# x - mean instead of the normalized x through both FFNs of a macaron block, and POOL's and TensorE's orders around it

## The reference

```python
x = x + 0.5 * ffn(layernorm(x))     # x: 4 x 256 tokens, 512 wide
x = x + attention(layernorm(x))     # 32 query heads, 8 key heads of 128, window of 128, rope
x = x + 0.5 * ffn(layernorm(x))     # the same weights again

layernorm(x) = (x - mean) / sqrt(var + 1e-5)
# ffn(xf), xf: 1024 x 512
probs = softmax(xf @ W_router.T)                 # 8 experts
w     = the two largest probs, divided by their sum, 0 elsewhere
h     = einsum("td,erd->ter", xf, lora_A)        # rank 16
lora  = einsum("ter,eor,te->to", h, lora_B, w) * 2.0
ffn   = xf @ W_base.T + b_base + lora
```

## Time and profile before

| | us |
|---|---|
| median of 3 runs | 746.47 (746.28 to 747.5) |
| the profiled execution | 746.33 |
| its span | 744.6 |
| TensorE busy in it | 717.2 (96%) |
| VectorE busy | 601.0 (81%) |
| ScalarE busy | 413.3 (56%) |
| POOL busy | 396.5 (53%) |
| mean granted TensorE clock | 0.998 of full |

### The profile page before, as it was taken

How to read it: one execution, slowest core, us unless ns; L and a number is a source line. 1 busy time by engine, 2 the same in 40 slices (tenths; PEclk the granted TensorE clock), 3 DMA queues, 4 the chain that set the end, 5 groups by cost and what they waited for, 6 DMA issues and landing times.

```text
span 744.6 us, 13949 instructions
## 1 busy us (share of the span) xinstructions
PE 717.2 (96%) x3692; PEld 603.1 (81%) x3692; DVE 601.0 (81%) x2060; ACT 413.3 (56%) x1122; POOL 396.5 (53%) x466
## 2 busy tenths in 40 slices
PE   8899789999999999999999999999999999998998
PEld 5787667888888888888888888888888888887786
DVE  6898778877887888878887888788878887788795
ACT  3324475657655676556655766576656665754320
POOL 0674268634864477438653765367535863462420
PEclk9999999999999999999999999999999999999999
DMA  8240003100220022002200120013000310030002
GB/s 266 73 158 16 0 3 98 43 1 2 73 70 1 0 70 70 0 0 70 56 14 0 56 70 14 0 32 94 15 0 0 99 28 1 1 114 1 0 31 85
DMA packets 25843, 32.13 MB, mean 43 GB/s; under 512 B 5833, under 2 KB 14281, under 8 KB 25298
## 3 DMA queue, kind: packets, MB, share of 16 engines
q1 hardware_dynamic: 25232, 30.69, 13.1%
q10 hardware_dynamic: 578, 1.05, 0.4%
HBM read 27.54 MB, written 4.19 MB: 43 GB/s over the span
## 4 chain that ended last, share of the span: by engine, by line
PE 70%; DVE 20%; issue 5%; ACT 3%; DMA 1%; POOL 1%; DVEq 0%; SPq 0%; ACTq 0%
PE bank L1102 26%; PE bank L1160 19%; PE bank L1145 6%; PE bank L1124 5%; PE bank L1068 5%; PE bank L1132 3%; DVE prob L822 2%; DVE rot L787 2%; DVE oT_lo L834 2%; DVE prob L814 1%; DVE sm L807 1%; PE bank L1121 1%; DVE rot L778 1%; ACT prob L550 1%; DVE pT_hi_lo L828 1%
## 5 line engine op out<-in xcount | busy, mean ns | idle before, releaser
L368 POOL TENSOR_TENSOR swap<-swap,rope 128x512 f32<-128x512 f32 x80 | 110.1, 1377 | 129.8 <-ACT swap L523 129.8
L550 ACT ACTIVATE prob<-sm,nmax 128x128 f32<-128x128 f32 x128 | 51.5, 403 | 151.4 <-DVE prob L814 150.4
L375 POOL TENSOR_SCALAR_AFFINE_SELECT pT_hi_lo<-pT_hi_lo 128x256 fp32r<-128x256 f32 x128 | 52.3, 409 | 140.3 <-DVE pT_hi_lo L828 139.8
L523 ACT ACTIVATE swap<-bank 64x512 f32<-64x512 f32 x160 | 94.9, 593 | 10.6 <-PE bank L1102 6.7
L558 ACT ACTIVATE pT_hi_lo<-bank 128x256 fp32r<-128x256 f32 x128 | 48.9, 382 | 71.5 <-PE bank L1132 50.6
L822 DVE TENSOR_SCALAR prob<-prob,rinv 128x128 f32<-128x128 f32 x256 | 83.3, 367 | 4.5
L385 POOL TENSOR_TENSOR q_lo<-rot,q_hi 128x512 fp32r<-128x512 f32 x64 | 82.6, 1291 | 6.9 <-ACT q_hi L531 6.9
L1160 PE MATMUL bank<-wo_hi,oT_hi 128*128 128x512 f32 x256 | 74.6, 413 | 5.0 <-DVE x L841 5.0
L828 DVE TENSOR_TENSOR pT_hi_lo<-bank,pT_hi_lo 128x256 fp32r<-128x256 f32 x128 | 53.6, 418 | 29.4 <-ACT pT_hi_lo L558 29.2
L1102 PE MATMUL bank<-xnT_hi,wq_hi 128*128 128x512 f32 x256 | 71.4, 391 | 2.2 <-DVE v_lo L798 1.4
L1102 PE MATMUL bank<-xnT_lo,wq_hi 128*128 128x512 f32 x256 | 73.4, 389 | 0.0
(11 more groups left out here) (150 smaller groups left out, 1768.9 us busy)
## 6 DMA issues: line engine op xcount, KB each, us to landing
raw<-in_L_attn_wq SPq DMA_DIRECT2D x32, 256.0 KB, 3.0
raw<-in_L_attn_wo SPq DMA_DIRECT2D x32, 256.0 KB, 2.6
x<-in_L_attn_x SPq DMA_DIRECT2D x4, 512.0 KB, 7.3
raw<-in_L_attn_wk SPq DMA_DIRECT2D x8, 256.0 KB, 2.7
raw<-in_L_attn_wv SPq DMA_DIRECT2D x8, 256.0 KB, 2.6
out<-x SPq DMA_DIRECT2D x8, 256.0 KB, 2.0
raw<-in_L_ffn_W_base ACTq DMA_DIRECT2D x4, 256.0 KB, 5.1
wb_keep_hi<-q_hi SPq DMA_DIRECT2D x1, 1024.0 KB, 4.9
```

The lines of the kernel that those rows point to most:

```text
L368: nc.gpsimd.tensor_tensor(w, w, tab, ALU.mult).then_inc(t2_done, 1)
L523: last = nc.scalar.activation(swap[a:a + half, m % 2, :], A[m % 2][b:b + half, :], ACT.Copy)
L550: last = nc.scalar.activation(prob[:, s % 2, lo:hi], src, ACT.Exp, bias=nmax[:, s % 2, i:i + 1], scale=-1.0, accum_out=rsum[:, s % 2, i:i ...
```

## The change

In both FFNs `xn` only subtracts the mean. The inverse deviation, positive for each token, comes back in two places: as the scale of the router's exponential, exp(rstd * (logit - top)), which becomes one activation per tile and waits for POOL's `rstd_done` (`RSTD_AT`), and as the scale of the last operation `ffn_out`. The half that stood there goes into W_base (`scale=0.5` in its copy, and in the low half), and the factor 2 of the LoRA part, halved too, is gone from h. The attention norm is as it was.

With it the orders change. POOL now makes the deviations of tiles 0 and 1 and of 2 and 3 as well, and that of tiles 4 to 7 ahead of the biases of tiles 0 to 3; in the last FFN it makes that of tiles 4 to 7, between the biases of tiles 3 and 4, in VectorE's place. TensorE transposes tiles 0 and 1 of x ahead of W_base, takes dense of pair 0 pass by pass for both tiles (`dense_by_pass`, the two passes with the high half of W_base first), and transposes tiles 2 and 3 ahead of h. VectorE does the statistics of tiles 2 and 3 behind the low half of W_base, and their subtraction ahead of the first router. ScalarE copies W_base in one go behind the x copies.

```diff
@@ -232,6 +232,8 @@
         def wo_lo(g, i):
             return 10 * g + 7 + i
 
+        RSTD_AT = ((1, 2, 3, 3), (6, 7, 8, 8))
+
         def rstd_steps(engine, then, t0, t1):
 
             vr, y, a, b = var[:, t0:t1], rstd[:, t0:t1], nt1[:, t0:t1], nt2[:, t0:t1]
@@ -410,9 +412,11 @@
                             rope_lo(2 * g + hf + 1, split, 1 - hf)
                         weights(g, hf, s, last)
 
+            norm_rstd(0, 0, 2)
+            norm_rstd(0, 2, 4)
+            norm_rstd(0, 4, NT)
             for t in range(NT // 2):
                 bias(0, t)
-            norm_rstd(0, 4, NT)
             split_lo(0, 0, wk_s[0][:, :, :], wk_s[1][:, :, :])
             for i in range(KT):
                 split_lo(1 + i, (1 + i) % RING, wq_s[0][:, i, :], wq_s[1][:, i, :])
@@ -432,6 +436,8 @@
             group(KV - 1, False, True)
             p_part(16 * KV - 1, SLOTS - 1)
             for t in range(NT):
+                if t == NT // 2:
+                    norm_rstd(2, 4, NT)
                 bias(1, t)
 
 
@@ -454,7 +460,7 @@
             def prepare_dense(lo, hi):
                 for d in range(lo, hi):
                     act.wait_ge(prep_tr, 3 + d)
-                    nc.scalar.activation(wb[0][:, d, :], bank[4 + d][:, :], ACT.Copy).then_inc(prep_hi, 1)
+                    nc.scalar.activation(wb[0][:, d, :], bank[4 + d][:, :], ACT.Copy, scale=0.5).then_inc(prep_hi, 1)
 
             def prepare_lora_b():
                 act.wait_ge(prep_tr, 7)
@@ -485,7 +491,11 @@
                 act.wait_ge(esub_done, p + 1)
                 if p == 0:
                     act.wait_ge(preset, 3)
-                nc.scalar.activation(ebuf[:, pr % 2, :, 0:EXPERTS], esub[:, :, :], ACT.Exp).then_inc(e_done, 1)
+                act.wait_ge(rstd_done, RSTD_AT[f][pr])
+                for i in range(2):
+                    t = 2 * pr + i
+                    last = nc.scalar.activation(ebuf[:, pr % 2, i, 0:EXPERTS], esub[:, i, :], ACT.Exp, scale=rstd[:, t:t + 1])
+                last.then_inc(e_done, 1)
 
             def split_hi(n, slot, count, dst):
                 act.wait_ge(raw_landed[slot], 16 * count)
@@ -594,10 +604,9 @@
             act.wait_ge(warm_ready, 1)
             nc.scalar.activation(rsum[:, 0, 0:1], sm[:, 0, 0:1], ACT.Exp)
             prepare_router()
-            prepare_dense(0, KT // 2)
             x_hi(0, 0)
             x_hi(0, 1)
-            prepare_dense(KT // 2, KT)
+            prepare_dense(0, KT)
             for pr in range(NT // 2):
                 if pr == 1:
                     prepare_lora_b()
@@ -679,16 +688,16 @@
                 dve.wait_ge(aggr, NT * ln + t1)
                 rstd_steps(nc.vector, then, t0, t1)
 
-            def norm(ln, t0, t1):
-                for t in range(t0, t1):
-                    norm_stats(ln, t)
-                norm_rstd(ln, t0, t1)
-
             def xn(ln, t):
                 i = NT * ln + t
                 wait(dve, tr_done, i - 1)
-                nc.vector.tensor_scalar(xn_buf(ln, t), x[:, t, :].rearrange("p (a n) -> p a n", a=2), mv[:, t, 0:1], rstd[:, t:t + 1],
-                                        ALU.subtract, ALU.mult).then_inc(xn_done, 1)
+                dve.wait_ge(aggr, i + 1)
+                src = x[:, t, :].rearrange("p (a n) -> p a n", a=2)
+                if ln == 1:
+                    ins = nc.vector.tensor_scalar(xn_buf(ln, t), src, mv[:, t, 0:1], rstd[:, t:t + 1], ALU.subtract, ALU.mult)
+                else:
+                    ins = nc.vector.tensor_scalar(xn_buf(ln, t), src, mv[:, t, 0:1], None, ALU.subtract)
+                ins.then_inc(xn_done, 1)
 
             def x_lo(ln, t):
                 i = NT * ln + t
@@ -731,9 +740,8 @@
                                              einv[:, :].unsqueeze(2).broadcast_to([P, 2, EXPERTS]), ALU.mult))
                 for i in range(2):
                     h = sm[:, i, 0:ER].rearrange("p (e r) -> p e r", e=EXPERTS)
-                    last = nc.vector.scalar_tensor_tensor(
-                        h, h, 2.0,
-                        wgt[:, i, :].unsqueeze(2).broadcast_to([P, EXPERTS, RANK]), ALU.mult, ALU.mult)
+                    last = nc.vector.tensor_tensor(h, h, wgt[:, i, :].unsqueeze(2).broadcast_to([P, EXPERTS, RANK]),
+                                                   ALU.mult)
                 last.then_inc(hw_done, 1)
 
             def ht_lo(f, pr):
@@ -747,7 +755,7 @@
                     t = 2 * pr + i
                     dve.wait_ge(out_done, NT * f + t + 1)
                     dve.wait_ge(biased, NT * f + t + 1)
-                    nc.vector.scalar_tensor_tensor(x[:, t, :], OUTB[f][pr % 2][i][:, :], 0.5, x[:, t, :],
+                    nc.vector.scalar_tensor_tensor(x[:, t, :], OUTB[f][pr % 2][i][:, :], rstd[:, t:t + 1], x[:, t, :],
                                                    ALU.mult, ALU.add).then_inc(x_out, 1)
 
             def prepare_router():
@@ -762,8 +770,8 @@
             def prepare_dense():
                 for d in range(KT):
                     dve.wait_ge(prep_hi, 3 + d)
-                    nc.vector.tensor_tensor(wb[1][:, d, :], bank[4 + d][:, :], wb[0][:, d, :].bitcast(F32),
-                                            ALU.subtract).then_inc(prep_lo, 1)
+                    nc.vector.scalar_tensor_tensor(wb[1][:, d, :], bank[4 + d][:, :], 0.5, wb[0][:, d, :].bitcast(F32),
+                                                   ALU.mult, ALU.subtract).then_inc(prep_lo, 1)
 
             def prepare_lora_b():
                 dve.wait_ge(prep_hi, 7)
@@ -849,7 +857,6 @@
                     dve.wait_ge(sum_done, 5 * 2 * KV)
                     dve.wait_ge(vt_done, 2 * KV)
                 if s in (2, 7):
-                    dve.wait_ge(rstd_done, 5 if s == 7 else 4)
                     xn(2, 2 if s == 7 else 0)
                     xn(2, 3 if s == 7 else 1)
                 if s == 3:
@@ -888,19 +895,19 @@
 
 
             nc.vector.memset(sm[:, 0, :], 0.0).then_inc(warm_ready, 1)
-            norm(0, 0, 2)
+            norm_stats(0, 0)
+            norm_stats(0, 1)
             xn(0, 0)
             xn(0, 1)
             prepare_router()
-            norm_stats(0, 2)
-            norm_stats(0, 3)
             x_lo(0, 0)
             x_lo(0, 1)
             prepare_dense()
-            router(0, 0)
-            norm_rstd(0, 2, 4)
+            norm_stats(0, 2)
+            norm_stats(0, 3)
             xn(0, 2)
             xn(0, 3)
+            router(0, 0)
             prepare_lora_b()
             ht_lo(0, 0)
             x_lo(0, 2)
@@ -913,7 +920,8 @@
                 if pr == 1:
                     router(0, pr)
                 if pr != 2:
-                    dve.wait_ge(rstd_done, 1 + pr // 2)
+                    if ln == 1:
+                        dve.wait_ge(rstd_done, 4)
                     xn(ln, t)
                     xn(ln, t + 1)
                 if pr > 1:
@@ -926,7 +934,7 @@
                     xn(0, 6)
                     xn(0, 7)
                 if ln == 1:
-                    dve.wait_ge(rstd_done, 3)
+                    dve.wait_ge(rstd_done, 5)
                     xn(1, 2)
                     xn(1, 3)
                 if ln == 1:
@@ -948,7 +956,8 @@
             norm_stats(1, NT - 1)
             rope_sum(0, 1)
             rope_cos(0, 2)
-            norm_rstd(1, 4, NT)
+            dve.wait_ge(aggr, 2 * NT)
+            rstd_steps(nc.vector, then, 4, NT)
             xn(1, 4)
             xn(1, 5)
             rope_sum(0, 2)
@@ -982,7 +991,6 @@
             x_add(4 * KV - 1, BATCH - 1, 1)
             norm_stats(2, 6)
             norm_stats(2, 7)
-            norm_rstd(2, 4, NT)
             for pr in range(1, NT // 2):
                 if pr > 1:
                     ht_lo(1, pr - 1)
@@ -1017,6 +1025,8 @@
                     last = tp(bank[3][:, d * EXPERTS:(d + 1) * EXPERTS], rot[0:EXPERTS, 1, d * P:(d + 1) * P],
                               ident[0:EXPERTS, 0:EXPERTS])
                 last.then_inc(prep_tr, 1)
+                x_transpose(0, 0)
+                x_transpose(0, 1)
                 for c in range(OUT // P):
                     pe.wait_ge(w_landed[c], 16)
                     for d in range(KT):
@@ -1067,6 +1077,15 @@
                     a, b = PASSES[n]
                     mm(OUTB[f][pr % 2][i][:, :], xnT[a][:, d, (2 * pr + i) * P:(2 * pr + i + 1) * P], wb[b][:, d, :],
                        start=(n == 0 and d == 0), stop=False)
+
+            def dense_by_pass(f, pr, order):
+
+                for n in order:
+                    a, b = PASSES[n]
+                    for i in range(2):
+                        for d in range(KT):
+                            mm(OUTB[f][pr % 2][i][:, :], xnT[a][:, d, (2 * pr + i) * P:(2 * pr + i + 1) * P], wb[b][:, d, :],
+                               start=(n == 0 and d == 0), stop=False)
 
             def h_transpose(f, pr):
                 p = 4 * f + pr
@@ -1198,19 +1217,17 @@
 
 
             prepare()
```

(8 more changed lines are left out.)

## The result

The changed kernel takes 750.94 us (median of 4 runs, 750.69 to 751.82), the kernel before 746.99 beside it (746.28 to 747.61). The ratio is 1.0050, 95% interval 1.0036 to 1.0065: slower by 0.5%. 747.6 was forecast, with a range that ended at 748.9. The profiled execution took 750.69, span 749.0 against 744.6, so 4.4 us are to be found.

The account below looks back on a forecast made before the run. TensorE was taken to bound the whole run, and POOL's queue to decide the changed front: +1.5 us at the projections and -0.3 at the end gave +1.2, forecast 747.6 us, range 745.0 to 748.9.

Parts of the forecast that it names:

- The step that failed: First FFN: pair 2 to the attention transposes keeps its 11.2 us, so TensorE is through at about 49.7.
- POOL's queue: First FFN: POOL runs without a gap from 27.5 and has the attention norm's first deviation at 52.5 instead of 49.39.
- the subtractions of tiles 6 and 7: First FFN, from 34.4 on: beside POOL's work the two tiles take 2.88 us, against 1.00 without it.
- the splits beside the router of pair 2: Slower rival, first FFN: POOL's biases and splits run longer, biases by 0.4 to 1.0 us; 748.1 to 749.0 us, chance 0.26.
- POOL's gate as what decides: Before the attention norm: VectorE waits for POOL's deviation at 52.5, so tile 0 is normalized 1.4 us later than before.
- The sum of five durations: POOL's queue from 27.5: chain 4.1, biases 5.02, splits 6.75, biases 5.18, chain 3.97, ending at 52.5.
- the very sign that the text named as proof against itself: At the attention norm: VectorE asking for tile 0 later than POOL has it would prove the forecast wrong.
- The stand and the clock: Ahead of the attention transposes: TensorE stands 3.4 us, then the clock falls to half and loses 1.0 to 1.7 us.
- The exponential: Each of 8 routers: the activation pair with pointer scale costs 0.17 us more, on the path only in a few.
- The estimate of 0.35: Router exponential: alternative cost of 0.35 instead of 0.17 us, from about 93 ns per pointer operand; sum 0.2 higher.
- The end: Last FFN: first router adds 0.17, the 0.32 gap before 720.84 closes; sum -0.3 us, between -0.35 and +0.1.
- The lead of 3.1 us at dense of pair 2: First FFN: dense of pair 2 forecast to start near 38.4 instead of 41.72, a lead of 3.3 us.

Follow-up runs that it names:

- e1_bias_first: The changed kernel with POOL's first four biases put back ahead of the deviation chain for tiles 4 to 7: 744.66 us, ratio 0.9969.
- e4_late_bias: The changed kernel with POOL's first four biases ahead of the chain of tiles 4 to 7, biases of tiles 4 to 7 behind the attention norm's deviations: 744.54 us.
- e2_order_alone: The kernel before, with only POOL's chain of tiles 4 to 7 moved ahead of the biases of tiles 0 to 3: 752.25 us, ratio 1.0065.
- e8_dummy_memset: e4_late_bias with 20 unused POOL memsets of 128x256 beside VectorE's router of pair 2: 751.23 us in one run.
- e11_fill_18: The changed kernel with 18 zero-matrix matmuls in TensorE's 4.87 us stand ahead of the h transposes of pair 2: 749.41 us, ratio 1.0039.
- e3_stt: The changed kernel with the h products in the old three-operand form, factor 1.0: 751.99 us, ratio 1.0066.
- e9_fill: The changed kernel with 20 zero-matrix matmuls in TensorE's stand ahead of the h transposes of pair 2, matrix cleared at the start: 750.17 us, ratio 1.0037.
- e12_fill_tail: e6_tail_hold with six zero-matrix matmuls in TensorE's stand ahead of the h transposes of pair 0 of the last FFN: 743.55 us, ratio 0.9963.
- e6_tail_hold: e4_late_bias with POOL's last-FFN biases of tiles 4 to 7 held until the h products they would lie beside are done: 744.93 us, ratio 0.9967.

## Why the prediction was wrong

**The step that failed** is in the paragraph on POOL's queue: "Pair 2 to the attention transposes took 11.2 us (41.72 to 52.95), so TensorE is through at about 49.7". It took 17.5 us (38.58 to 56.11). The duration of before was carried over, although the same paragraph had just moved POOL's splits and biases from 33.40 to 45.33 on to 36.7 to 48.4, that is onto the whole of VectorE's router of pair 2, whose last part had been free of them. The prediction knew the contention: it priced it for the subtractions of tiles 6 and 7 (2.88 forecast, 2.82 measured) and named "the splits beside the router of pair 2" in a rival, but there only as a loss of POOL's, 0.4 to 1.0 us. It was VectorE that lost, 4.7 us, and behind its stand TensorE lost 1.6 more to the clock. e1_bias_first and e4_late_bias take the overlap away, and the late gate with it (48.38 and 44.45), and end faster than before; e2_order_alone puts the order into the kernel before and loses there, with a gate that nobody waits for. The SBUF page of the Trainium skill ("SBUF: two separate sides") states it: a VectorE operation with two SBUF inputs blocks against a GpSimd one that reads, for the whole instruction. The runs agree for the products (0.49 beside memsets, 0.91 beside short additions, 2.57 beside long ones). The prediction read from that page of the Trainium skill only what bears on large operations; in the router five small ones each paid for the POOL instruction that they met.

**POOL's gate as what decides: wrong.** The sum of five durations was right to 0.14 us (52.5 against 52.36), with some luck: the first chain took 4.35 instead of 4.1, the splits 6.43 instead of 6.75, and such misses cancelled. But VectorE asked at 52.83, after it. That is the very sign that the text named as proof against itself. The queue was on time and did its harm on the way. The two paths lie close, though: with the router 4.7 us shorter VectorE would have asked near 48.1 (an estimate, 52.83 - 4.7) and stood for this gate as forecast, and e8_dummy_memset shows such a stand. No run has the free router with the gate left at 52.36, so how much the overlap alone adds to what the late gate would have cost stays open.

**The stand and the clock: right in kind.** 3.4 us of stand were forecast ahead of the attention transposes, 4.87 came ahead of the h transposes; the clock fell to 0.50 behind it, and the loss forecast at 1.0 to 1.7 measured 1.59 by rows, 1.5 by the rows of e11_fill_18. That a stand of about this length came at all was luck: another wait made it, at another place.

**The exponential: nearly right.** The pair took 0.49 (0.45 taken), VectorE idled 0.16 for it; TensorE's stand behind the first router of the last FFN grew by 0.26, against 0.17 forecast. The estimate of 0.35 from the page ScalarE: Activation LUTs of the Trainium skill ("What ACT_TABLE_LOAD costs") was too high, by its working: it put the pointers' price on top of the 0.45 of two copies of 128x136. The 93 ns per pointer of that page of the Trainium skill fit: one exponential of 128x8 with the pointer took 0.28 to 0.30, one of 128x16 without it 0.22.

**The end: wrong by two terms.** -0.3 was forecast for the closing gap. In e1_bias_first and e4_late_bias it stays, at 0.30 and 0.25: with the chain on POOL, biases 4 and 5 now start just when VectorE's h products do, the same overlap a second time (the products take 2.66). In the changed kernel the gap did close, but by luck: with the clock down the products started 0.2 ahead of the biases (722.23 and 722.45) and took 0.49. And the clock, which had stayed up here in the profile of before, fell behind the stand of 1.50 us: +1.38, not in the sum at all.

**What the change is worth.** The lead of 3.1 us at dense of pair 2 was real. Without the overlap 2.8 us of it reach the projections (57.51 against 60.31) and the kernel is 0.3% faster than before.

## What to carry to other kernels

When a change moves one engine's queue, lay the moved instructions over the other engine's timeline again before reusing any duration from it: a stage's length belongs to its neighbours too. On the queue that VectorE shares a path with, put long two-input operations beside VectorE's long waits or its work from PSUM, never beside a chain of small dependent steps with SBUF inputs; here one line's place in POOL's queue was worth 0.8%. A sum that comes out right to 0.1 us does not show that it is the sum that decides: find the last arrival at each meeting point.

## What the runs showed of the hardware

- A VectorE product of 128x128 with both inputs in SBUF (0.29 us alone) took 1.31 and 1.35 beside POOL additions of 128x512, 0.29 and 0.70 beside ones of 128x256, and 0.29 beside memsets. Each stretched one ended 0.03 to 0.16 us behind the POOL instruction that it met. A copy of 128x4 took 1.33 in two kernels (the changed one and e11_fill_18) and 0.16 in e2_order_alone and e3_stt; in all four it starts 0.01 to 0.02 us ahead of a POOL instruction, so the rows do not tell which way it goes.
- The granted clock fell behind TensorE stands as short as 1.02 us, but not every time. Behind the one of 1.02 or 1.03 us near 23 it fell in three of eleven profiles (e1_bias_first, e9_fill, e12_fill_tail), behind the one of 1.49 or 1.50 us in the last FFN in seven of ten; e4_late_bias kept it and e6_tail_hold lost it at that same place. Behind the four that lasted 3.0 us or more it fell each time. The medians of these kernels are therefore mixtures: eight of the ten runs of e4_late_bias lie at 743.5 to 744.9, two at 746.0 and 746.1. Why one execution loses it and the other does not, no run here settles.
